# A decoder layer's cross attention with the softmax sums moved behind the weighted values, and its entry and exit staged differently

## The reference

```
x = x + attention(layernorm(x)) @ w_out.T                  # 16 heads of 32, 2048 x 2048 scores a head
q = layernorm(x) @ Wq.T + bq                               # cross attention, context of 154 rows a batch
scores = einsum('bhtd,bhsd->bhts', q, k) * scale           # k, v = ctx @ Wk.T + bk, ctx @ Wv.T + bv
scores = where(causal_mask, neg_inf, scores); scores = where(key_padding_mask, neg_inf, scores)
x = x + (softmax(scores) @ v) @ Wo.T + bo
x = x + feed_forward(layernorm(x))                         # shared expert on all rows, 8 routed experts on 1024 rows
```

## Time and profile before

| | us |
|---|---|
| median of the three runs shown | 3276.14 (3267.62 to 3276.48) |
| the profiled execution | 3278.49 |
| its span, first to last instruction | 3276.7 |
| self-attention, until PE's last instruction | 330 to 2106 |
| queries stage | 2116 to 2354 |
| cross attention | 2354 to 2723 |
| shared feed forward | from 2723 |

### The profile page before, as it was taken

The page is one execution under the profiler, slowest core; times in us unless marked ns, Lnnn a source line. Parts: engine busy times, 40 slices in busy tenths (PEclk is TensorE's granted clock), DMA queues, the critical chain, the costliest instruction groups (busy, mean ns, idle before and its releaser), DMA issues. The chain is left out here.

```text
span 3276.7 us, 42067 instructions
## 1 busy us (share of the span) xinstructions
PE 2981.6 (91%) x15214; PEld 1748.8 (53%) x15214; DVE 2089.1 (64%) x3792; ACT 1611.7 (49%) x2996; POOL 1758.9 (54%) x728
## 2 busy tenths in 40 slices
PE   8999799999999999999999999699499995889488
PEld 5877355455555554555545554277364554777333
DVE  4332877777777777777777776156167694665323
ACT  2222166666666666666666667322055572222111
POOL 1000188898888988897988888600202002342265
PEclk9999599999999999999999999799787797999589
DMA  7444754745657456565474554378654232343621
GB/s 231 176 165 165 170 110 98 162 94 120 145 113 156 100 110 145 110 137 122 104 163 93 121 128 88 101 201 237 157 142 136 87 110 107 136 151 112 212 68 36
DMA packets 187062, 435.75 MB, mean 133 GB/s; under 512 B 30429, under 2 KB 51838, under 8 KB 166844
## 3 DMA queue, kind: packets, MB, share of 16 engines
q1 hardware_dynamic: 162742, 288.49, 30.5%
q0 software_dynamic: 24128, 144.75, 21.4%
HBM read 180.67 MB, written 127.18 MB: 94 GB/s over the span
## 5 line engine op out<-in xcount | busy, mean ns | idle before, releaser
L816 DVE TENSOR_REDUCE part_max<-ps_s 128x1 f32<-128x512 f32 x2048 | 1270.7, 683 | 355.1 <-PE ps_s L717 355.0
L916 ACT ACTIVATE probs<-ps_st 128x512 f32<-128x512 f32 x2048 | 1058.6, 602 | 505.0 <-PE ps_st L736 500.5
L666 POOL TENSOR_TENSOR added<-added,probs 128x2048 f32<-128x2048 f32 x256 | 1191.3, 4654 | 79.4 <-ACT probs L916 56.7
L736 PE MATMUL ps_st<-q_stack,k_stack 98*128 98x512 f32 x2048 | 867.5, 427 | 7.3 <-ACT probs L916 6.0
L717 PE MATMUL ps_s<-k_stack,q_stack 96*128 96x512 f32 x2048 | 829.1, 411 | 32.7 <-POOL max_parts L656 20.7
L736 PEld LDWEIGHTS ps_st<-q_stack,k_stack 98*128 98x128 f32 x2048 | 388.5, 190 | 519.1 <-ACT probs L916 359.7
L747 PE MATMUL ps_pv<-probs,v_sb 128*32 128x512 f32 x4096 | 550.5, 610 | 0.0
L717 PEld LDWEIGHTS ps_s<-k_stack,q_stack 96*128 96x128 f32 x2048 | 397.7, 194 | 130.3 <-DVE part_max L816 45.7
L674 POOL DMA_DIRECT2D probs<-probs x128 | 111.1, 868 | 200.7 <-PE ps_pv L747 181.6
L1411 PE MATMUL xps_s<-xks_stack,xq_stack 99*128 99x154 f32 (+1 forms) x512 | 123.6, 321 | 52.9 <-DVE xident_r L1524 47.2
L747 PEld LDWEIGHTS ps_pv<-probs,v_sb 128*32 128x32 f32 x4096 | 80.9, 108 | 163.6 <-ACT probs L916 137.0
(11 more groups left out here) (269 smaller groups left out, 3627.4 us busy)
## 6 DMA issues: line engine op xcount, KB each, us to landing
probs<-probs POOLq DMA_DIRECT2D x128, 1024.0 KB, 6.9
xq_stack<-q_parts SPq DMA_DIRECT2D x64, 384.0 KB, 4.6
q_stack<-q_hi SPq DMA_DIRECT2D x64, 256.0 KB, 6.3
k_stack<-k_hi SPq DMA_DIRECT2D x64, 256.0 KB, 8.5
q_parts<-q_h_out SPq DMA_DIRECT2D x64, 256.0 KB, 4.9
x_in<-in_x_rows SPq DMA_DIRECT2D x8, 1024.0 KB, 7.2
q_hi<-qk_h_out SPq DMA_DIRECT2D x8, 1024.0 KB
q_lo<-qk_l_out SPq DMA_DIRECT2D x8, 1024.0 KB
```

Source lines behind the costliest of these rows:

```text
L666: pool.tensor_tensor(added[:, w % 2], left, probs[:, k % RING], ALU.add).then_inc(added_up, 1)
L736: pe.matmul(ps_st[:, n % BANKS], k_stack[0:TOP, w // BPB, j, k * P:(k + 1) * P], q_stack[:, w % 4, j], start=True, stop=True).then_inc(ite ...
L816: dve.tensor_reduce(part_max[:, s:s + 1], ps_s[:, (w * SLOTS + s) % BANKS], AX.X, ALU.max)\
L916: act.activation(probs[:, k % RING, j], ps_st[:, n % BANKS], ACT.Exp, scale=SCALE).then_inc(item_used, 1)
```

## The change

It has five parts, in the order of the stages.

A. `self_attention`: `INVERT_AT` goes from 7 to 9 and `PRODUCT_AFTER` from 4 to 5.

B. `attention_to_queries`: the query's parts get two buffers in turn (in the half of `k_stack` that is free there), so ACT and DVE wait for the store of two blocks before. SP stores the two copies of the high part as soon as it is there, then the low part. The last block's three parts go out from SP, ACT and POOL.

C. `cross_attention`, entry: four of the five fills go to DVE; POOL keeps the one of `xks_stack`. SP starts its loads at once; the padding rows are loaded later, and only scores of units that are not causal wait for them.

D. `cross_attention`, loop: PE's `totals(u - 1)` stands directly behind `weighted_values(u - 1)` at t = 4; ACT's `sums_out(u - 1)` stands ahead of exponential 6. The weights ahead come in five parts of two chunks (u = 6, 9, 12, 15, 18), split by POOL in pieces of 128x512. At u = 21 to 24 SP loads the first block of the feed forward (`ahead_raw`) and its residual rows (`first_x1`), eight DMAs; ACT splits off the high part after the last unit's exponentials, DVE the low part at u = 32 ahead of the last units' reciprocals.

E. `shared_feed_forward`: the first block is neither loaded nor split here; PE's first projection starts without a wait, POOL adds the bias to `first_x1`, and the residual waits tile by tile. POOL still adds the bias to block 1 ahead of its first `e_rstd`.

```diff
-    INVERT_AT = 7
-    PRODUCT_AFTER = 4
+    INVERT_AT = 9
+    PRODUCT_AFTER = 5
...
+        def store_part(engine, i, u, s, stored):
+            for r in range(P // HD):
+                engine.dma_start(q_blocks[2 * i + u][s, r // 2, r % 2], q_out[r * HD:(r + 1) * HD, u, s % 2].bitcast(F32))\
+                      .then_inc(stored, 16)
...
                     sp.wait_ge(group_high, count(i, u, DC, DC))
-                    sp.wait_ge(group_low, count(i, u, DC, DC))
-                    for h in range(2):
-                        for j in range(2):
-                            r = (2 * h + j) * HD
-                            for s, src in enumerate((q_h, q_l, q_h)):
-                                sp.dma_start(q_blocks[2 * i + u][s, h, j], src[r:r + HD].bitcast(F32)).then_inc(q_stored, 16)
+                    store_part(sp, i, u, 0, q_stored[u])
+                    if not last:
+                        store_part(sp, i, u, 2, q_stored[u])
+                        sp.wait_ge(group_low, count(i, u, DC, DC))
+                        store_part(sp, i, u, 1, q_stored[u])
...
-                        if g == 0 and not first(i, u):
-                            act.wait_ge(q_stored, count(i, u, 16 * Q_DMAS, 0))
-                        act.activation(q_h[:, g], ps_g[:, g], ACT.Identity, bias=bq_sb[:, g:g + 1]).then_inc(group_high, 1)
+                        if g == 0 and not (isinstance(i, int) and i == 0):
+                            act.wait_ge(q_stored[u], i * (16 * Q_DMAS))
+                        act.activation(q_out[:, u, 0, g], ps_g[:, g], ACT.Identity, bias=bq_sb[:, g:g + 1]).then_inc(group_high, 1)
...
-                sp.wait_ge(ones_set, 2)
                 load_q(0)
                 load_scores_k(0)
...
-                sp.wait_ge(ones_set, 4)
                 load_q(1)
                 load_transposed_k(0)
+                sp.wait_ge(rows_set, 1)
...
                     elif u in AHEAD_AT:
-                        ahead.load(sp, AHEAD_AT.index(u))
+                        n = AHEAD_AT.index(u)
+                        if n >= 2:
+                            sp.wait_ge(ahead_low, 2 * (n - 1))
+                        sp.dma_start(ahead_raw[:, n % 2], PARTS[n][0]).then_inc(ahead_loaded[n % 2], 16)
+                    elif NEXT_AT <= u < NEXT_AT + 4:
+                        c = u - NEXT_AT
+                        if c == 0:
+                            sp.wait_ge(ahead_low, 2 * len(PARTS))
+                            for s in range(2):
+                                sp.wait_ge(out_stored[s], 16 * QUADS // 2)
+                        sp.dma_start(ahead_raw[:, c // 2, c % 2],
+                                     attn_t.rearrange("b (c p) (n k) -> b n c p k", p=P, k=BLK)[0, 0, c]).then_inc(next_loaded, 16)
+                        sp.dma_start(next_x[:, c], x1_rows.rearrange("(n t p) d -> n t p d", t=TPB, p=P)[0, c])\
+                          .then_inc(next_loaded, 16)
...
+                pool.memset(ks_stack[ROWS:TOP + 1].bitcast(F32), 0.0).then_inc(ones_set, 1)
+                for n, (_, high, low) in enumerate(PARTS):
+                    pool.wait_ge(ahead_loaded[n % 2], 16 * (n // 2 + 1))
+                    for c in range(2):
+                        pool.tensor_copy(high[:, c], ahead_raw[:, n % 2, c]).then_inc(ahead_high, 1)
+                    for c in range(2):
+                        pool.wait_ge(ahead_high, 2 * n + c + 1)
+                        pool.tensor_tensor(low[:, c], ahead_raw[:, n % 2, c], high[:, c].bitcast(F32), ALU.subtract)\
+                            .then_inc(ahead_low, 1)
...
                         if t == BEFORE_VALUES and exists(u - 1):
                             weighted_values(u - 1)
+                            totals(u - 1)
                         if exists(u):
                             transposed_scores(u, t)
                         if exists(u + 2):
                             scores(u + 2, t)
-                    if exists(u - 1):
-                        totals(u - 1)
...
+                dve.memset(mk[:], 0.0).then_inc(rows_set, 1)
+                dve.memset(q_stack[ROWS:TOP + 1].bitcast(F32), 1.0).then_inc(rows_set, 1)
+                dve.memset(kt_stack[ROWS:TOP].bitcast(F32), 1.0).then_inc(rows_set, 1)
+                dve.memset(ones[:], 1.0).then_inc(rows_set, 1)
                 dve.wait_ge(consts_loaded, 48)
...
                 for u in range(UNITS + 2):
+                    if u == UNITS:
+                        dve.wait_ge(next_high, 1)
+                        dve.tensor_tensor(next_l, ahead_raw[:].rearrange("p a c d -> p (a c) d"), next_h.bitcast(F32), ALU.subtract)\
+                           .then_inc(next_low, 1)
...
+                        if t == BEFORE_VALUES + 2 and exists(u - 1):
+                            sums_out(u - 1)
                         if exists(u):
                             exponentials(u, t)
-                    if exists(u - 1):
-                        sums_out(u - 1)
+                    if u == UNITS - 1:
+                        act.wait_ge(next_loaded, 128)
+                        act.activation(next_h, ahead_raw[:].rearrange("p a c d -> p (a c) d"), ACT.Copy).then_inc(next_high, 1)
...
+                    if not first(i, u):
+                        pool.wait_ge(loaded[u], i * (16 * LOADS) + 16 * LOADS * u)
+                    rows = first_x if first(i, u) else x_in[:, u]
                     for t in range(TPB):
-                        pool.tensor_tensor(x_in[:, u, t], x_in[:, u, t], bo_all[:], ALU.add).then_inc(bo_added, 1)
+                        pool.tensor_tensor(rows[:, t], rows[:, t], bo_all[:], ALU.add).then_inc(bo_added, 1)
...
+                project(0, 0)
                 pe.wait_ge(w_loaded, 6 * 16)
                 pe.wait_ge(bias_low, 1)
                 pe.wait_ge(consts, 5)
-                project(0, 0)
```

More of the change, by code:

```diff
@@ L49, in stage_semaphores @@
     return sem
[L52 to L74, removed]
 def weight_rows(w):
@@ L996, in attention_to_queries @@
         group_done, group_high, group_low = (sem(f"c_{n}") for n in ("group_done", "group_high", "group_low"))
-        q_stored = sem("q_stored")
+        q_stored = [sem(f"q_stored{s}") for s in range(2)]
+        last_stored = sem("q_last_stored")
         x1_stored = [sem(f"x1_stored{s}") for s in range(2)]
@@ L1285, in cross_attention @@
         ps_d = ctx.enter_context(nc.psum_tensor("xps_d", [P, BLK], F32))
-        ahead = Ahead(sem, weights_ahead, [sb(f"xahead_raw{n}", [P, high.shape[1], D])[:]
-                                           for n, (_, high, _) in enumerate(weights_ahead)])
+        ahead_raw = sb("xahead_raw", [P, 2, 2, D])
+        PARTS = [(source[:, c:c + 2], high[:, c:c + 2], low[:, c:c + 2])
+                 for source, high, low in weights_ahead for c in range(0, high.shape[1], 2)]
+        ahead_loaded = [sem(f"xahead_loaded{s}") for s in range(2)]
+        ahead_high, ahead_low, next_loaded, next_high, next_low = (
+            sem(n) for n in ("xahead_high", "xahead_low", "xnext_loaded", "xnext_high", "xnext_low"))
         ks_loaded, kt_loaded = ([sem(f"x{n}_loaded{b}") for b in range(B)] for n in ("ks", "kt"))
-        v_loaded = sem("xv_loaded")
+        v_loaded, padding_loaded = sem("xv_loaded"), sem("xpadding_loaded")
         q_loaded = [sem(f"xq_loaded{s}") for s in range(BUFS)]
         consts_loaded, masks_loaded = sem("xconsts_loaded"), sem("xmasks_loaded")
-        ones_set, ident_ready = sem("xones_set"), sem("xident_ready")
+        ones_set, rows_set, ident_ready = sem("xones_set"), sem("xrows_set"), sem("xident_ready")
         scores_done, max_done = sem("xscores_done"), sem("xmax_done")
@@ L1360, in _ @@
                 sp.dma_start(v_sb[:], xv_rows).then_inc(v_loaded, 16)
+                sp.wait_ge(ones_set, 1)
+                for b in range(B):
+                    load_padding(b)
                 for u in range(UNITS + 3):
@@ L1381, in _ @@
                     sp.wait_ge(out_stored[s], 16 * UNITS // 2)
+                sp.wait_ge(next_loaded, 128)
             @block.gpsimd
             def _(pool):
-                for n, (tile, value) in enumerate(((q_stack[ROWS:TOP + 1].bitcast(F32), 1.0), (ks_stack[ROWS:TOP + 1].bitcast(F32), 0.0),
-                                                   (kt_stack[ROWS:TOP].bitcast(F32), 1.0), (mk[:], 0.0),
-                                                   (ones[:], 1.0))):
-                    if n:
-                        pool.wait_ge(ones_set, n)
-                    pool.memset(tile, value).then_inc(ones_set, 1)
-                pool.wait_ge(ones_set, 5)
-                for step in range(ahead.STEPS):
-                    ahead.split_step(pool, step)
-                pool.wait_ge(ahead.low_done, len(weights_ahead))
+                pool.memset(ks_stack[ROWS:TOP + 1].bitcast(F32), 0.0).then_inc(ones_set, 1)
[7 more added lines that the diff above has]
+                            .then_inc(ahead_low, 1)
```

(9 more changed lines are left out.)

56 lines of the change are left out of this document (33 added, 23 removed).

## The result

The changed kernel takes 3406.99 us (median of 4 runs, 3402.01 to 3407.48) against 3275.85: a ratio of 1.0403, interval 1.0384 to 1.0422. It is slower, as forecast, but by 131 us and not by 50, outside the stated range. Times are medians; one of the four executions of experiment 1 took 6045 us and is left out of its median.

The account below looks back on a forecast made before the run. It took TensorE and DVE, both nearly full in cross attention, and the clock as deciding: 3278.5 - 20 - 5 - 8 + 26 + 64.5 + 3.5 + 3 - 14 = 3328.5, so 3326 us at the median; range 3237 to 3346.

Parts of the forecast that it names:

- hand-made period of 9.9: Cross attention loop: a unit without mask takes 9.9 us at full clock in the new order, +1.6 a unit.
- the clock holds: Rival for the cross attention loop: stops are short, the clock stays full, 3239 us, down to 3216; chance 0.23.
- both D rows: Cross attention from TensorE's first matmul: to the last xattn_raw, forecast +94; from there to the feed forward's entry, +3.
- 2 x 9.9 + 10 x 14.5: First 12 cross attention units without mask: two at full clock, ten at half clock, 165 us against 139.0, +26.
- +0.5 a masked unit: Cross attention's masked units: mask matmuls give TensorE more to do, so the new order costs 7 x 0.5 = +3.5 us.
- The product moves one add later with it, and nothing waits for it within the unit.: Self-attention, part A: the later product was given no cost, within a term of -20 us, bounds 0 and -23.
- Expectation 1: Stated ahead of experiment 1: TensorE no longer stops, two links issued together delay the sums' small transfer; 3302 us (+26).
- A frees nothing: Rival in self-attention: another wait at the turns or a late product, +20 us; chance 0.06 under low clock, or worse.
- What goes is TensorE's 12.0 us.: Self-attention's quad turns: TensorE's 12.0 us of waits vanish, with part of the half clock following; -20 us taken.
- B, C and E: Forecast terms for the query's store, the fills at cross attention's entry and the feed forward's entry: -5, -8, -14 us.
- the slope I chose: Cross attention's entry: DVE fills at 1.05 ns an element, 16 us in all, first matmul at 16.3, -8 us.
- forecast path: Feed forward's entry: POOL's eight bias adds of 1.67 us hold back e_rstd, at +19.6 against +33.8, -14 us.

Follow-up runs that it names:

- experiment 1: Kernel before with part A alone (INVERT_AT 9, PRODUCT_AFTER 5): 3301.14 us, ratio 1.0116.
- Experiment 2: Kernel before with only the loop's new order of totals and sums, weights still in whole tiles: 3406.20 us, ratio 1.0419.
- 3: Changed kernel with totals and sums put back where they were before: 3243.03 us, ratio 0.9909.
- 4: Changed kernel with the order of totals and sums and also part A undone: 3224.52 us, ratio 0.9865.
- experiment 5: Changed kernel without DVE's reciprocals of cross attention's sums, the values multiplied by the sums as they are: 3251.57 us (one run).
- experiment 6: Version of 4 with one more, useless reciprocal of 256 columns a unit on DVE ahead of the product: 3372.49 us (one run).
- 11: Version of 4 with the totals at t = 6, two tiles behind the values, sums still copied at the end: 3391.12 us (one run).
- 12: Changed kernel with each transposed score matmul of units without mask issued twice into the same bank: 3387.38 us (one run).
- experiment 7: Kernel before with INVERT_AT 9 alone, the product where it was: 3274.72 us, ratio 0.9999.
- Experiment 9: Kernel before with PRODUCT_AFTER 5 alone, the reciprocal where it was: 3321.34 us, ratio 1.0153.
- 10: Kernel before with part A, SP issuing the q, k, v loads ahead of its wait for the product and the store: 3275.11 us, ratio 1.0002.

## Why the prediction was right and wrong

**Right: the loop's mechanism, its direction, and that the clock decides.** DVE dry for 2 us, the stop ahead of the values, a fall that no half-clock unit lifts, 14.7 a unit (14.86 measured), full clock again as the masked units begin: as the steps said. Experiment 2 shows that the order alone does it, 3 and 4 that it takes the order, 5 and 6 that it goes by way of DVE's lateness and TensorE's stop. The hand-made period of 9.9 at full clock was not seen in a unit without mask, since none ran at full clock; those at full clock, all masked or next to masked ones, took 9.7 to 11.5. The rival "the clock holds" is out, and with it, in this kernel, the Trainium skill's rule (TensorE: Matmul & The Clock Gate, "Why this matters for your kernels") of gaps of about 3 us: in the loops of before, of the changed kernel and of experiments 2, 5, 6, 11 and 12 the falls came during a stop of 1.04 to 1.6 us or within 2.5 us after it, except two: that of experiment 5 above, and the second of experiment 2, at 2683.86, early in a stop of 0.76 us.

**Mis-sized: the loop, +131.6 for +97** (the sum of both D rows). The term "2 x 9.9 + 10 x 14.5" let the clock fall one or two units into each stretch. It fell in the last unit of the masked group (2441 to 2453), whose scores ahead are already those of units without mask: the first 12 units took 180.1 us (forecast 165), the last 12 169.1 (160), and the masked units cost 16.5 more (4.5 in the first group, 12.0 in the second, in which the clock fell twice) where I had 3.5. Two units at 14.86 in place of 9.9 are 9.9 us in each stretch; the rest of the first is its other ten at 15.0 in place of 14.5. I took +0.5 a masked unit from the mask matmuls' extra work and forgot that the last ones share their loop pass with units that have none.

**Failed: "The product moves one add later with it, and nothing waits for it within the unit."** This term stood at nothing, and A measured +26 for -20. SP waits for the product. SP's queue, in order, is: the wait for the product, the store of `attn_out`, then the next unit's q, and at a quad turn 3 MB of k and 1 MB of v. Product and loads at the first turn, before:

```profile
597.60 1.57 POOL L683 TENSOR_TENSOR attn_out<-attn_out,attn_raw 128x512 f32<-128x512 f32 x1
...
601.60 0.33 SPq L577 DMA_DIRECT2D q_stack<-q_hi  x1
...
609.68 0.43 SPq L589 DMA_DIRECT2D v_sb<-v_rows  x1
...
630.58 0.35 SPq L599 DMA_DIRECT2D dens_c<-dens_rows  x1
...
632.47 0.33 SPq L602 DMA_DIRECT2D recip_rows<-recip_c  x1
```

and in the changed kernel:

```profile
600.07 1.27 POOL L658 TENSOR_TENSOR attn_out<-attn_out,attn_raw 128x512 f32<-128x512 f32 x1
...
601.36 0.34 SPq L587 DMA_DIRECT2D attn_t<-attn_out  x1
...
601.74 0.43 SPq L552 DMA_DIRECT2D q_stack<-q_hi  x1
...
611.67 0.42 SPq L564 DMA_DIRECT2D v_sb<-v_rows  x1
...
620.69 7.18 SPq L572 DMA_DIRECT2D dens_rows<-dens_sb  x1
...
630.04 1.78 POOL L649 DMA_DIRECT2D probs<-probs  x2 [4.33 <-DMA probs<-probs]
...
631.66 0.35 SPq L574 DMA_DIRECT2D dens_c<-dens_rows  x1
...
642.36 0.34 SPq L577 DMA_DIRECT2D recip_rows<-recip_c  x1
```

The two kernels' times here are compared from the end of the unit (attn_raw), 607.11 before and 604.56 after. Before, the product ends at 599.2, ahead of the point at which q may be loaded, 601.60, which is 5.5 us before the unit's end. Now it ends at 601.34, and only then can SP go on: q is issued 2.8 us before the unit's end, v 7.1 us behind it where it was 2.6. The sums' first 8 KB transfer, dens_rows, is issued 16.1 us into the unit in both. But until the second, dens_c, which waits for its landing, it takes 11.0 us where it took 7.4: dens_c is issued at 631.66, 27.1 us into the unit where it was 23.5, and now stands behind two links that POOL has just issued, 2 MB. It takes 10.4 us from issue to landing, where the median of all units is 1.7; in experiment 7 it is issued ahead of both links and takes 1.6. So the reciprocals leave at 642.36, 37.8 us into the unit where it was 25.4 (28.9 in experiment 7, which inverts them as late). In experiment 1, whose turn is the same, two windows show what that does:

```profile
610.00:615.00 5.00, 5.00 (x28) 2.89 (x30) 3.97 (x7) 3.70 (x8) 4.86 (x2) 1.00 0.98 233
...
635.00:640.00 5.00, 0.64 (x8) 0.23 (x8) 0.54 (x1) 0.00 (x0) 4.49 (x1) 0.89 1.04 212
```

The DMA engines are full from 610 to 640, and in the last 5 us of it TensorE is busy for 0.64. (Before, they are full until 630; from 630 to 635 their share is 0.62.) Experiment 9 shows that the product alone does it, 10 that it goes by SP's order: with that edit alone, 3301 becomes 3275 us and the ratio to the kernel before 1.0002. I had named what waits on DVE and not what is queued behind the waiting instruction on SP. Expectation 1 had the collision with the links right, but its cause, TensorE no longer stopping, was refuted by 7. The rival "A frees nothing" named a late product, but priced it at a lost gain of 20 us and not at a loss.

**Failed too: "What goes is TensorE's 12.0 us."** The wait went, and no time with it. In experiment 7 the reciprocal waits for nothing and TensorE no longer waits for the maxima, but it waits 18.2 us for the link of the chain sums:

```profile
PE ps_d L755 <- DMA probs<-probs: 18.2, 13, 3.2
```

By the shares above the turns are bound by the DMA engines: TensorE meets the same transfers at the next place where it needs one; the turn units sum to 27.0 us over six quiet ones (52.12 each), before 23.5. The prediction's count of the clock's falls there was off too: three of the six stops had one (at 633, 1268 and 1487), not two.

**B, C and E: right to a microsecond, two of them by luck.** B: last matmul to first store went from 5.71 us to 0.75. C: DVE's fills run at 0.84 ns an element (6.88 us for 8192), POOL's rate and not the slope I chose; two gaps of 1.8 and 1.0 us between them, which the trace puts down to issue, made up for it. By the Trainium skill's cycle an element (VectorE: DVE Perf Modes, "Zero memsets can be issued as uint32 (trn2)") I estimate 1.04 ns at the clock it gives; the row is quicker. The zero fill of bf16 ran as 1024 elements of uint32, which that section says is possible (0.91 us). E: e_rstd came at +20.0 (2886.19 - 2866.21) (forecast 19.6), but not by the forecast path: POOL was done in time (2885.5) and waited for DVE; TensorE had stopped 2.71 us for the residual, which stands behind the bias split on DVE, and POOL's later adds take 1.25 us each where I used 1.67.

## What to carry to other kernels

Where TensorE and a second engine are both nearly full, the long block that needs nothing of the second engine belongs over that engine's other work; moved by half a unit it cost an estimated 1.6 us a unit at full clock and, with the clock, 6.6 as measured (14.86 against 8.27), so a stop of a microsecond in a loop is to be priced at both clock levels, and the neighbouring units looked at for where the fall starts. Before an operation is made later, read the in-order queue of every engine that waits for it down to the next big transfer: here a product some 5 us later put off 4 MB of loads by up to 4.5 us, and these an 8 KB transfer that then took 10.4 us. A wait that vanishes where transfers are the bound only moves to the next consumer.

## What the runs showed of the hardware

One stop does not decide. In the changed kernel a stop of 1.25 us ahead of 2438.79 left the clock at 1.00 and one of 1.56 ahead of 2449.37 didn't; in experiment 6 1.22 passed and 1.61 didn't, in experiment 11 1.08 passed and 1.27 didn't; but in experiment 12 1.17 passed and 1.04 didn't, and in the self-attention of before, of the six stops of 1.45 to 2.84 us behind the earlier trace rows three passed, one of 2.37 us among them. In experiment 5 the clock fell with no stop above 0.54 us. So the length of the stop is not all; what else counts stays open. Once at 0.50, the changed kernel's units without mask, with TensorE busy 95% and more, never raised it; units with mask matmuls did, each time, and the doubled wide matmuls of experiment 12 sometimes.
